# Two graph layers on one core: late chunks of the first sums reordered, the last group of the second sums in halves, ring and side buffers of the second gathers exchanged

## What is computed

```python
def gat_conv(h, src, dst, fc_w, attn_l, attn_r, bias, heads, out_feats):
    feat = (h @ fc_w.T).reshape(n, heads, out_feats)
    el, er = sum(feat * attn_l, -1), sum(feat * attn_r, -1)
    e = leaky_relu(el[src] + er[dst], 0.2)
    ex = exp(e - segment_max(e, dst)[dst])
    a = ex / segment_sum(ex, dst)[dst]
    return segment_sum(feat[src] * a[..., None], dst) + bias
# layer 0: norm = 1 / clip(degree, 1)
h0 = gat_conv(x, ..., heads=8, out_feats=32)                 # first pass over the edges
h1 = relu(h0 + norm * (x @ wb0.T + bb0))
h2 = gat_conv(h1, ..., heads=1, out_feats=256)               # second pass
x = layernorm(x + h2 + norm * (concat(x, h1) @ wb1.T + bb1))
# layer 1: attention with keys, values and 64 edge types, 4 heads (third pass), then layernorm
```

## Time and profile before

| | us |
|---|---|
| median of 3 runs (lowest, highest) | 2234.57 (2231.80, 2241.07) |
| the profiled execution, its own time | 2232.32 |
| its span, first to last instruction | 2230.6 |
| gathers of the first pass on POOL | 75.9 to 612.0 |
| POOL waits | 612.0 to 706.65 |
| gathers of the second pass on POOL | 706.65 to 1278.7 |
| end of `sum2`, `node3` | 1278.7 to 1344.8 |
| third pass and end | 1344.8 to 2230.6 |

### The profile page before, as it was taken

How to read it: one execution, slowest core, us unless ns; L and a number is a source line. 1 busy time by engine, 2 the same in 40 slices (tenths; PEclk the granted TensorE clock), 3 DMA queues, 4 the chain that set the end, 5 groups by cost and what they waited for, 6 DMA issues and landing times. The chain is left out here.

```text
span 2230.6 us, 29002 instructions
## 1 busy us (share of the span) xinstructions
PE 1509.1 (68%) x7673; PEld 1137.5 (51%) x7674; DVE 1516.2 (68%) x2333; ACT 404.5 (18%) x735; POOL 1273.5 (57%) x1321
## 2 busy tenths in 40 slices
PE   6247567566566444886666599778777875599965
PEld 4235455455445443775455446555555554477743
DVE  3357877777775886773434376676767667698968
ACT  1100000000014001000000053443434442100124
POOL 0477777777702887577777706777777773000023
PEclk9657778778787555998877899877778777799989
DMA  3644444444405564344444428999999998577412
GB/s 99 161 133 128 127 120 128 123 123 125 111 11 170 173 173 135 106 129 118 119 119 118 123 104 270 342 345 335 344 343 339 339 339 286 196 273 272 168 43 74
DMA packets 234905, 406.10 MB, mean 182 GB/s; under 512 B 33199, under 2 KB 171621, under 8 KB 228197
## 3 DMA queue, kind: packets, MB, share of 16 engines
q0 software_dynamic: 73216, 219.89, 31.6%
q1 hardware_dynamic: 161637, 185.66, 26.3%
HBM read 330.93 MB, written 74.48 MB: 182 GB/s over the span
## 5 line engine op out<-in xcount | busy, mean ns | idle before, releaser
L840 POOL DMA_INDIRECT row_space<-tab_feat,src_i x760 | 742.8, 977 | 312.2 <-issue 230.9
L1088 PE MATMUL ps<-arena 128*128 128x257 f32 (+1 forms) x1664 | 429.5, 419 | 148.2 <-DVE arena L1933 148.2
L840 POOL DMA_INDIRECT row_space<-tab_kv,src_i x416 | 393.3, 945 | 192.6 <-issue 123.1
L1088 PEld LDWEIGHTS ps<-arena 128*128 128x128 f32 x1664 | 340.6, 210 | 230.7 <-issue 171.8
L1187 PE MATMUL ps<-arena 128*128 128x265 f32 x832 | 262.1, 482 | 115.3 <-DVE ps L2172 56.5
L1927 DVE TENSOR_TENSOR arena<-row_space,ps 128x2048 f32<-128x2048 f32 x95 | 216.6, 2280 | 161.6 <-DMA row_space<-tab_feat,src_i 161.6
L1022 PE MATMUL ps<-acc,arena 128*128 x832 | 285.6, 502 | 0.0
L1187 PEld LDWEIGHTS ps<-arena 128*128 128x128 f32 x832 | 197.1, 243 | 168.4 <-issue 123.1
L1420 ACT COPY acc<-ps 128x265 f32<-128x265 f32 (+2 forms) x75 | 28.2, 376 | 1149.3 <-PE ps L1088 580.4
L1806 DVE TENSOR_TENSOR arena<-row_space,ps 128x1024 f32<-128x1024 f32 x104 | 126.8, 1219 | 139.8 <-PE ps L1022 78.0
L1022 PEld LDWEIGHTS ps<-acc,arena 128*128 128x128 f32 x832 | 195.5, 246 | 38.0
(11 more groups left out here) (337 smaller groups left out, 2132.2 us busy)
## 6 DMA issues: line engine op xcount, KB each, us to landing
item_v<-row_space SPq DMA_DIRECT2D x52, 1024.0 KB, 8.2
row_space<-item_v SPq DMA_DIRECT2D x52, 1024.0 KB, 4.9
arena<-rows_block_dst SPq DMA_DIRECT2D x104, 128.0 KB
row_space<-tab_feat,src_i POOLq DMA_INDIRECT x760, 2.8
scores<-rows_block_dst SPq DMA_DIRECT2D x52, 128.0 KB
arena<-rows_src_low SPq DMA_DIRECT2D x52, 128.0 KB
row_space<-tab_kv,src_i POOLq DMA_INDIRECT x416
arena<-rows_type SPq DMA_DIRECT2D x52, 128.0 KB
```

What stands on the lines that cost most here:

```text
L840: nc.gpsimd.indirect_dma_start(rows_of_slot(s)[:, g, :], None, table, bass.IndirectOffsetOnAxis(ap=src_i[:, item:item + 1], axis=0),).then ...
L1088: last = nc.tensor.matmul(ps[:, SUM_BANKS:2 * SUM_BANKS][:, bass.ds(bs[g], 1), 0:width].rearrange("p a d -> p (a d)"), onehot[:, s % 2, g, ...
```

## The change

1. **First sums, order.** Chunks 10 and 11 both use `sums_first` (PE and DVE). The terms of chunk 12, made in `period(10)` before, are now made in `sums_first(11)`, one group after another, and DVE makes the logits of chunk 12 after them.
2. **First sums, last one-hots.** The four sets of one-hots of chunk 12 are written to a place of their own (`last_onehot`, in the rows of chunk 11) between the steps of its softmax, not in its `build`.
3. Eight products into a bank that nothing reads (`WARM`) stand on PE between `carries(12)` and `shares(12)`.
4. **node2.** DVE begins it without waiting for PE and ACT: the inverses of blocks 0 to 19 wait for 20 copied blocks, those of 20 to 24 for all. DVE's loop is unrolled.
5. **Second gathers.** Side buffers 0 to 5 take groups 0 to 5, the ring takes groups 6 to 13, side buffers 6 to 8 take groups 14 to 16, and the ring goes on with 17. The order of the items is the same.
6. **Second sums, last group.** The first four items of group 51 signal apart, and are weighted and summed ahead of the other four; six unread products (`WARM_HALF`) stand between the halves on PE.

```diff
+LAST_ONEHOT_AT = 12288
+WARM_HALF = 6
+WARM = 8
...
-                for k in range(first):
-                    gather_early(k)
-                for i in range(mine):
-                    gather(i // ring, i % ring)
+                if n == 1:
+                    for k in range(AHEAD):
+                        gather_early(k, k)
+                for i in range(ring):
+                    gather(i // ring, i % ring, (AHEAD if n == 1 else 0) + i)
+                if n == 1:
+                    for k in range(AHEAD, EARLY):
+                        gather_early(k, ring + k)
+                for i in range(ring, mine):
+                    gather(i // ring, i % ring, first + i)
...
-                        pe.wait_ge(weighted_made, u * SLOTS + (s + 1 + n * GROUPS))
+                        halved = n == 1 and ends and s == SLOTS - 1
+                        if not halved:
+                            pe.wait_ge(weighted_made, u * SLOTS + (s + 1 + n * GROUPS))
                         for g in range(GROUP):
+                            if halved and g == 0:
+                                pe.wait_ge(last_half_weighted, 1)
+                            if halved and g == GROUP // 2:
+                                for _ in range(WARM_HALF):
+                                    nc.tensor.matmul(ps[:, RESIDUAL_BANK, 0:D], ident[:], w_b[:, 1, :], start=True, stop=True)
+                                pe.wait_ge(weighted_made, GROUPS + GROUPS)
...
-                def sums_first(c):
+                def sums_first(c, terms=False):
                     pe.wait_ge(sum_mm, c * CHUNK_COUNT + CREDIT)
                     for s in range(SLOTS):
                         if s % 2 == 0:
                             banks, cleared = sum_banks(c, s)
+                            if terms:
+                                pair = term_blocks(c + 1, s)
                         group_sums(c, s, banks, cleared)
+                        if terms:
+                            term_products(c + 1, s, pair)
                     transposed(c + 1)
                     lane_ends(c + 1)
                     carries(c + 1)
+                    if terms:
+                        for _ in range(WARM):
+                            nc.tensor.matmul(ps[:, TERM_BANK, 0:D], ident[:], w_b[:, 0, :], start=True, stop=True)
                     shares(c + 1)
                     factors(c + 1)
...
-                with nc.tensor.Fori(0, CHUNKS - 3) as u:
+                with nc.tensor.Fori(0, CHUNKS - 4) as u:
                     period(u + 1, False, False, True)
-                sums_first(CHUNKS - 2)
+                sums_first(CHUNKS - 3)
+                sums_first(CHUNKS - 2, True)
...
-                def sums_first(c, half, turn):
+                def sums_first(c, half, turn, last):
                     rescale(c)
                     for g in range(1, SLOTS):
                         build(c, half, g)
+                        if last:
+                            next_terms(c + 1, 1 - half, g - 1, False)
+                    if last:
+                        next_terms(c + 1, 1 - half, SLOTS - 1, False)
+                        item_onehots(last_onehot[:, 0], c + 1, 0)
+                        dve.wait_ge(score_read[1], nth(c + 1, SLOTS - 1) + 2)
                     make_logits(c + 1, turn + half, 1 - half)
-                    soft_chunk(c + 1)
+                    if last:
+                        item_onehots(last_onehot[:, 1], c + 1, 1)
+                    lane_tops(c + 1)
...
-            begin(dve, "node2", ["pe", "act"])
-            did(vec.tensor_copy(deg[:].unsqueeze(2), acc[:, :, DEG:AW]))
-            inverses(H1, 0, 1)
-            inverse_degrees(0, 1)
+            def degrees_and_inverses(lo, hi):
+                dve.wait_ge(sum_copied, hi)
+                did(vec.tensor_copy(deg[:, lo:hi].unsqueeze(2), acc[:, lo:hi, DEG:AW]))
+                inverses(H1, lo, hi)
+                inverse_degrees(lo, hi)
```

More of the change, by code:

```diff
@@ L838, in gather @@
                     for g in range(GROUP):
-                        item = (first + u * ring + s) * GROUP + g
+                        item = group * GROUP + g
+                        first_half = n == 1 and group == GROUPS - 1 and g < GROUP // 2
                         nc.gpsimd.indirect_dma_start(
@@ L1895, in sums @@
                     dve.wait_ge(weights_in[2], 3 * 16)
[L1896 removed]
+                ring = RINGS[nth_pass]
+                ahead = EARLY + ring if nth_pass == 1 else 0
                 turns, rest = (GROUPS - ahead) // ring, (GROUPS - ahead) % ring
@@ L1914, in build @@
                         ALU.is_equal)
-                    if u is None and i < ahead:
-                        dve.wait_ge(early_in[i], 16 * GROUP)
-                        taken = early_rows[i]
+                    kept = u is None and nth_pass == 1 and (i < AHEAD or ring + AHEAD <= i < ahead)
+                    if kept:
+                        k = i if i < AHEAD else i - ring
+                        dve.wait_ge(early_in[k], 16 * GROUP)
+                        taken = early_rows[k]
                     elif nth_pass == 3:
@@ L1930, in build @@
                                              ALU.mult)
-                    if not (u is None and i < ahead):
+                    if not kept:
                         made.then_inc(slot_used[s], 1)
```

81 lines of the change are left out of this document (55 added, 26 removed).

## The result

The changed kernel takes 2212.93 us (median of 4 runs, 2212.04 to 2214.87) against 2235.4 for the kernel before, run beside it (4 runs, 2231.8 to 2241.07). The ratio is 0.9898, with a 95% interval from 0.9876 to 0.9921: faster by 22.5 us, or 18 to 28. The profiled execution took 2214.87, the longest of the four; its span is 2213.1. Span against span the gain is 17.5 us.

The account below looks back on a forecast made before the run. POOL was taken to set the second pass. First sums +8.6, node2 -6.5, stall -12.1 and halves -4.6 gave -14.6 from 2232.32, so 2217.7; with 2.25 to the median, 2220.0 us, range 2214 to 2226.

Parts of the forecast that it names:

- step (c): First sums, chunk 11: term products and register reads lengthen the four groups' 17.96 us; PE ends at 631.9, not 627.6.
- Step (a): First sums: chunk 10, summed as chunk 11 was, takes 37.2 us from rescale to rescale, not 40.2; gain 3.0.
- Step (b): First sums, PE's start of chunk 11: a second register read behind the same wait costs 2.0 us.
- Rival (2): The first stretch costs more, through a clock fall in chunk 11 and SP in node2: total -9.6, 2225 us; chance 0.16.
- (d): First sums: chunk 12's logits wait for DVE's last term reads, residual and one-hots; 3.3 us in all, 7.8 later.
- (e): First sums: three more one-hot sets in softmax waits add 1.8 us and save 0.75 before chunk 12's first weighting.
- (f): First sums, last chunk: PE at the low clock ends at 671.0 (+8.6), at the high clock 668.6 (+6.2).
- from there SP sets the pace: node2 from the fifth product: SP's stores take 29.6 us for 21 blocks, so nothing more is gained.
- safety of 2.2 us: Second gathers, group 17: DVE weights group 6 2.2 us before POOL needs its slot, so the 12.1 us stall goes.
- Rival (1): The first stretch costs nothing: products keep the clock up or the second read is hidden; about 2216.5 us; chance 0.20.
- (3): Second gathers: the stall does not go, as group 6 is weighted too late; with half of it, 2226 us; chance 0.04.
- (4): First sums, chunk 11: PE and DVE fall into lockstep, +23 us, total +8.6, 2243 us; chance 0.04.

Follow-up runs that it names:

- first_only: Kernel before with only the whole edit of the first sums, its last one-hots and eight unread products included: 2244.32 us, ratio 1.0015.
- after_half_warm0: Changed kernel without the six unread products between the halves of the second sums' last group: 2214.42 us, ratio 0.9899.
- old_first_reads_warm: Changed kernel with the old first sums, chunk 11's bank reads ahead of the wait, and unread products in three waits of PE: 2204.30 us, ratio 0.9856.
- reads_warm_late: Changed kernel with register reads of chunks 10 and 11 ahead of the wait and four more unread products before chunk 12's sums: 2208.27 us, ratio 0.9881.
- ring_only: Kernel before with only the side buffers 6 to 8 moved to groups 14 to 16 of the second gathers: 2226.65 us, ratio 0.9942.
- halves_only: Kernel before with only the last group of the second sums in halves, with its six unread products: 2234.43 us, ratio 0.9976.
- `_only`: Four kernels, each the kernel before with one part of the change (second gathers, halves, node2, first sums): ratios 0.9942, 0.9976, 0.9975, 1.0015.
- after_reads_ahead: Changed kernel with the register reads of chunks 10 and 11 issued before the wait for the rescale: 2210.98 us, ratio 0.9885.

## Why the forecast was wrong, and where it was right

Two steps failed. One is a term of the sum: step (c), the four groups of chunk 11, was put at 23.25 us and took 20.44. The other is the step from the sum to the median: it was put at +2.25 us and was -1.94. The mechanisms held otherwise.

Means over the profiles of the table make the sum again: the kernels with the old form of a part against those with the new one. Kernels in which another edit changes the stretch are left out: those with moved reads for the first sums, first_only for the old node2 (the new one is taken behind the new first sums), after_half_warm0 for the tail, old_first_reads_warm for node3.

| term | forecast | measured |
|---|---|---|
| first sums | +8.6 | +5.2 (94.9 to 100.1) |
| node2 | -6.5 | -7.8 (44.1 to 36.3) |
| stall | -12.1 | -13.2 (571.7 to 558.5) |
| tail | -4.6 | -3.9 (11.9 to 8.0) |
| node3 | 0 | +0.6 (53.9 to 54.5) |
| total | -14.6 | -19.1 |

**First sums: the term that was most wrong**, by 3.4 us (3.9 in the pair of profiles), and its mechanism was right: the last term product does gate the last softmax (the DVE row at 628.95), and the transposes of chunk 12 come 4.0 us later behind chunk 10's rescale than before (64.2 for 60.2 us). Step (a) holds: 36.7 us from rescale to rescale for 37.2. Step (b) holds: a second read costs 1.6 (3.73 less 2.15), for 2.0. Step (c) failed. It took the four groups at 17.96 us, with their time at the low clock, and put 5.3 on top: 23.25. They took 20.44 (608.48 to 628.92). The first group took 5.32 and not 6.7, because the granted clock rose 3.0 us behind its start (at 611.5), and before 5.8 us behind it (at 615.4). Why it rose earlier is not shown, and in reads_warm_late the same group took 6.88 again. The two reads in the middle left PE idle for 1.08 us and not for 2.20, as in the period's row; why is open too. The rest is 0.3 us. Rival (2) had expected the clock of this place to err to the other side. Steps (d) and (e) hold to 0.4 us (3.3 and 18.3 for 3.3 and 18.65), and (f) to 0.1: it begins at the low clock and takes 17.2 us for 17.1.

**The unread products.** Right for the eight: no gain. The prediction's clock times in the earlier trace rows are a little off: by the shares of the two windows the fall is at 632.5 and the rise at 649.6, not 632.8 and 649.3. Between the eight and the sums PE had only small products of 0.8 us in all, and was idle for 2.6 us before them and 3.2 us after; the sums began at the low clock. By the Trainium skill, "TensorE: Matmul & The Clock Gate", HAM oscillation, a PE that has idled starts its next burst at half rate; the trace agrees. old_first_reads_warm shows the other side of it: a clock that is kept up to the work is worth 1.5 us in the last chunk.

**node2** gave 1.3 us more. The head was right (fifth product 6.25 us behind the sums, for 6.5). What was off is "from there SP sets the pace" at 29.6 us: it took 28.3, 1.34 us a block, within the bounds of 4 and 8 that were given. The 29.6 held one store of 1.67 us, where its neighbours take 0.37. The seven profiles without such a store take 28.3 from the fifth block on, the six with one 28.9 to 29.6. Why a store is slow is not shown.

**The stall** went as said; the 12.1 of the profile of before was the smaller end. In the four kernels that have the stall, it is 12.1, 12.0, 14.1 and 12.8 us. The safety of 2.2 us was not there in ring_only, which lost only hundredths by it.

**The tail.** 7.0 was said, 7.4 was seen, and the mean of eight is 8.0, because the six unread products can stand in the way of the last four items. The bound of 0.2 us for them was the mistake (2.6 in halves_only).

**The base.** In the pair of profiles the sum is 17.5 us for 14.6: 2214.87, where 2217.7 was said. That is 2.8 of the 7.1 us by which the forecast missed. The other 4.2 are the step from the profile to the median: the forecast added 2.25, since the profile of before lay so far under its median, and the median of the changed kernel lies 1.94 under its profile. No row gave this step for the changed kernel, and which execution is profiled is a draw; why it came out the other way is not shown. The terms by the means make 19.1 us, the medians 22.5. The profile of before was a good one: its node3 took 52.3 us where the four `_only` kernels, with the same code there, took 53.7 to 55.0, and the medians of before in the other three sessions were 2236.5 to 2241.9. The interval of the result, 18 to 28, holds the 19.1. The four `_only` kernels, by their ratios, add up to -0.92%, the change is -1.02%: the parts make the whole within the noise. What of the last 3 us is in the change and what is in the draw of the runs stays open.

Rival (1), "the first stretch costs nothing", gave 2216.5 and came nearest in time, but not by its reasons: neither did the products keep the clock up nor was the second read hidden. Rivals (2), (3) and (4) did not come. (3) was closer than its chance of 0.04 says.

## What to carry to other kernels

Look at what an engine does between a wait and its work: reads of registers that stand behind the wait are paid in full (1.6 to 2.2 us each here) and cost nothing in front of it. Moving them brought 5.6 us. The new order is, by the stretches, a loss with the reads in either place. Unread products are worth their place only if they run up to the work they are meant for: with 6.7 us between them and the work they brought nothing, with 2.3 us the clock held, and where the work is ready they are a delay (2.6 us in halves_only). And of a profile of one execution, each stage is a draw: before a term of 2 us is taken from it, it is worth knowing whether the same stage in a second profile has the same length. The same goes for the distance of one profiled execution from the median.

## What was not expected of the hardware

The same code meets the clock in different ways. The first group of chunk 11 took 5.32, 5.28 and 6.88 us in the changed kernel, after_reads_ahead and reads_warm_late, of which the last two are alike up to there; node3's first products took 1.98 to 3.78 us, and the whole stage 52.3 to 55.1. In the stage behind it, where the DMA engines are busy for nearly all of the time (a DMA share of 0.99 to 1.00 in the windows from 1370 to 1800 us in before), and behind it, the program took from 884 to 893 us, with no part of it changed. And one store of SP in node2 took 0.98 to 1.73 us in six of the thirteen profiles, where the like ones take 0.34 to 0.37.
